# Attention and mixture-of-experts block on one core: row sums moved between buffers, normalising on GpSimd, long projections in two parts

## The reference

```python
q = X @ Wq.T + bq ; k = ctx @ Wk.T + bk ; v = ctx @ Wv.T + bv
w = softmax(where(masks, -inf, q k / sqrt(16)))        # 32 heads, 256 x 256
x = x + tanh(g_xattn) * ((w v) @ Wo.T + bo)            # X is the layernorm of x
t = layernorm(x)
shared = (silu(t @ S1.T) * (t @ S3.T)) @ S2.T          # S1, S3: 512 to 256; S2 back
scores = sigmoid(t @ gate.T) ; top 2 of 8 experts (with bias)
x = x + tanh(g_ffn) * (shared + sum of the two chosen experts, bf16)
```

## Time and profile before

| | |
|---|---|
| median of 3 runs | 863.16 us (861.75 to 866.41) |
| the profiled execution | 858.97 us, span 856.9 us |
| mean granted clock of TensorE | 0.877 of 2.4 GHz |
| busy TensorE / VectorE / ScalarE / GpSimd | 693.1 / 469.0 / 291.4 / 68.7 us |
| first scores of body 0 | 67.5 us from the span's start |
| first VectorE multiply L817 of bodies 1 to 8 | 159.1, 230.1, 301.3, 369.0, 440.5, 511.5, 573.9, 632.3 us |
| expert phase | 669 to 857 us |

### The profile page before, as it was taken

How to read it: one execution, slowest core, us unless ns; L and a number is a source line. 1 busy time by engine, 2 the same in 40 slices (tenths; PEclk the granted TensorE clock), 3 DMA queues, 4 the chain that set the end, 5 groups by cost and what they waited for, 6 DMA issues and landing times. The chain is left out here.

```text
span 856.9 us, 14813 instructions
## 1 busy us (share of the span) xinstructions
PE 693.1 (81%) x4417; PEld 480.3 (56%) x4417; DVE 469.0 (55%) x1041; ACT 291.4 (34%) x601; POOL 68.7 (8%) x100
## 2 busy tenths in 40 slices
PE   0436999699599789869959969989637799999998
PEld 0335758477377568648737747657326344444443
DVE  4417665368458467555836846564223455555554
ACT  1121454244333344433524433443201333333332
POOL 7400001001001000100100100000102000000000
PEclk9965979789799989978979988859657899999999
DMA  4785464444535543553545462430236022222111
GB/s 149 171 228 103 109 159 125 80 103 138 113 97 119 130 100 102 147 86 85 155 81 119 118 129 49 103 84 26 90 74 111 25 62 62 62 62 62 49 48 50
DMA packets 65199, 84.84 MB, mean 99 GB/s; under 512 B 15176, under 2 KB 43664, under 8 KB 64912
## 3 DMA queue, kind: packets, MB, share of 16 engines
q1 hardware_dynamic: 61008, 77.58, 36.9%
q0 software_dynamic: 2304, 6.29, 3.9%
q10 hardware_dynamic: 1856, 0.57, 0.3%
HBM read 60.75 MB, written 29.70 MB: 106 GB/s over the span
## 5 line engine op out<-in xcount | busy, mean ns | idle before, releaser
L593 ACT ACTIVATE probs<-ps 128x512 f32<-128x512 f32 x256 | 147.2, 598 | 150.3 <-PE ps L936 149.9
L800 DVE TENSOR_REDUCE mx<-ps 128x2 f32<-128x512 f32 x256 | 172.6, 683 | 39.7 <-PE ps L917 39.3
L917 PE MATMUL ps<-kst,qst 65*128 65x256 f32 x512 | 127.9, 336 | 65.3 <-DVE mx L800 59.6
L917 PEld LDWEIGHTS ps<-kst,qst 65*128 65x128 f32 x512 | 96.4, 213 | 115.1 <-DVE mx L800 76.1
L1085 PE MATMUL ps_h<-w,q_sg 128*128 128x512 bf16 x512 | 132.8, 383 | 5.2 <-PEq L77 5.2
L936 PE MATMUL ps<-qst,kst 66*128 66x512 f32 x256 | 113.8, 447 | 2.3 <-ACT probs L593 1.1
L1136 DVE SCALAR_TENSOR_TENSOR hid<-ps_h,sc_in,up 128x256 bf16<-128x256 f32 x128 | 61.9, 484 | 87.1 <-ACT up L1126 86.1
L1126 ACT ACTIVATE up<-ps_h,sc_in 128x256 f32<-128x256 f32 x128 | 60.7, 475 | 120.1 <-PE ps_h L1085 120.1
L1085 PEld LDWEIGHTS ps_h<-w,q_sg 128*128 128x128 bf16 x512 | 49.9, 99 | 67.8 <-issue 10.5
L949 PE MATMUL psa<-probs,v_st 128*32 128x256 f32 x1024 | 77.9, 427 | 1.2 <-ACT probs L593 1.2
L1103 PE MATMUL ps_o<-probs,hidT 128*128 128x512 bf16 x256 | 76.2, 380 | 0.8 <-DVE hidT L1142 0.8
(11 more groups left out here) (126 smaller groups left out, 1071.7 us busy)
## 6 DMA issues: line engine op xcount, KB each, us to landing
qst<-q_d SPq DMA_DIRECT2D x96, 128.0 KB
q_d<-q_sg SPq DMA_DIRECT2D x32, 256.0 KB, 3.0
a_d<-a_sb SPq DMA_DIRECT2D x32, 256.0 KB, 2.2
x_n<-in_x SPq DMA_DIRECT2D x8, 512.0 KB, 4.0
c_raw<-in_ctxT SPq DMA_DIRECT2D x8, 512.0 KB, 3.4
w<-in_w13T POOLq DMA_DIRECT2D x8, 512.0 KB, 16.1
x<-in_x SPq DMA_DIRECT2D x8, 512.0 KB, 3.4
a_dn<-a_d SPq DMA_DIRECT2D x8, 512.0 KB
```

The source lines that it names most:

```text
L593: act.activation(probs[:, v % 8, :], ps2[v % 2][:, :, :].rearrange("p h q -> p (h q)"), ACT.Exp, scale=HD ** -0.5).then_inc(s_exp, 1)
L800: dve.tensor_reduce(mx[:, c % 2, 0:8 * NT].rearrange("p (h t) -> p h t", t=NT)[:, h:h + 2, w // 2], ps1[u % 2][:, :, :], AX_X, ALU.max)\
L917: last = pe.matmul(o[:, i, :], qst[0:ROW_MAX, c, h, t * P:t * P + P], kst[0:ROW_MAX, c, g % 2, :], start=(i == 0 or not masked), stop=not ...
```

## The change

Five things change together.

1. The sums no longer come back from DRAM. `move_sums` copies them from `a_sb` straight into `den`, two small transfers for each chunk, issued before that chunk's `store_a`.
2. The chain of normalising is cut in two halves of two chunks each. Half 0: values loaded and reciprocals stored in step 5, spread in step 9. Half 1: values in step 20, reciprocals (`store_r`, two transfers) in 21, spread in 23. VectorE takes reciprocals in steps 4 and 20.
3. The multiply and the low part move from VectorE to GpSimd (`normalise`, `low_values`), each on half the chunks; ScalarE takes the high part in steps 16 and 26.
4. H0, H1, G, W0 and W1 are each issued in two parts in different steps (`BEGUN` says where the first part stands). Both W parts wait for all of the normalised batch.
5. Items and transfers are put in other steps (K from 13 to 0, so the context is loaded a body earlier, at step 27; D, T and Q later; `store_q`, `load_stack` of the next batch at 24 instead of 22). Body 6 is written out, the loop runs over 2 to 5.

```diff
-PREP = [(11, "T0"), (12, "T1"), (13, "K"), (14, "Q0"), (16, "Q1"), (18, "Q2"), (20, "Q3"), (21, "V0"), (22, "V1")]
+PREP = [(0, "K"), (13, "T0"), (14, "T1"), (16, "Q0"), (18, "Q1"), (20, "Q2"), (21, "V0"), (22, "Q3"), (25, "V1")]
+FIRST = ["T0", "T1", "K", "Q0", "Q1", "Q2", "Q3", "V0", "V1"]
-TAIL = [(0, "MT3"), (29, "W0"), (30, "W1")]
-TAIL2 = [(1, "X0"), (2, "X1"), (4, "H0"), (5, "H1"), (6, "G"), (8, "D0"), (9, "D1")]
-ROUTE_AT, ROUTE_RATE = 9, 2
+TAIL = [(0, "MT3"), (29, "W0"), (31, "W1")]
+TAIL2 = [(1, "X0"), (2, "X1"), (5, "H0"), (8, "H1"), (10, "G"), (12, "D0"), (13, "D1")]
+BEGUN = {"H0": 4, "H1": 6, "G": 9, "W0": 28, "W1": 30}
+ROUTE_AT, ROUTE_RATE = 12, 2
...
+            def move_sums(b, c):
+                ready((s_aev, b * G + 2 * c + 2), (s_rd, b * 2 + c // 2 - 1))
+                for w in range(2):
+                    row = 32 * c + 16 * w
+                    sp.dma_start(den[row:row + 16, :], a_sb[HD:P:32, c % 2, w, :]).then_inc(s_den[c % 2], 16)
+
+            def load_values(b, h):
+                for i in range(2):
+                    ready((s_aw[i], b * 32 + 16 * h + 16))
+                ready((s_ln2, b * LN2))
+                sp.dma_start(a_dn[:, 2 * h:2 * h + 2, :].rearrange("p c q -> p (c q)"),
+                             a_d[b, :, 0:HD, 2 * L * h:2 * L * h + 2 * L]).then_inc(s_ar[h], 16)
...
+            def load_r(b, h):
+                ready((s_rw, b * 64 + 32 * h + 32), (s_ln2, b * LN2))
+                sp.dma_start(f(a_lo[:, 2 * h:2 * h + 2, :].rearrange("p c q -> p (c q)")),
+                             r_d[b, h].unsqueeze(1).broadcast_to([G, HD, 2 * L])).then_inc(s_rr[h], 16)
...
+            def normalise(b, h):
+                pool.wait_ge(s_rr[h], b * 16 + 16)
+                pool.wait_ge(s_ar[h], b * 16 + 16)
+                half = a_dn[:, 2 * h:2 * h + 2, :]
+                pool.tensor_tensor(half, half, a_lo[:, 2 * h:2 * h + 2, :].bitcast(F32), ALU.mult).then_inc(s_an, 1)
+
+            def low_values(b, h):
+                pool.wait_ge(s_ahi, b * 2 + h + 1)
+                pool.tensor_tensor(a_lo[:, 2 * h:2 * h + 2, :], a_dn[:, 2 * h:2 * h + 2, :],
+                                   a_hi[:, 2 * h:2 * h + 2, :].bitcast(F32), ALU.subtract).then_inc(s_alo, 1)
...
-                    if u in (27, 28) and prev:
-                        t = u - 27
-                        act.wait_ge(s_an, b * NT - NT + t + 1)
+                    if u in (16, 26) and prev:
+                        h = u // 26
+                        act.wait_ge(s_an, b * 2 - 2 + h + 1)
...
-                    pe.wait_ge(s_alo, b * NT + k + 1)
+                    if part == 0:
+                        pe.wait_ge(s_alo, b * 2 + 2)
...
+                            for name, begin in BEGUN.items():
+                                if begin == u and name in idx and not last:
+                                    item(name, b - 1 if name[0] == "W" else b - 2, idx[name], (par0 + par[name]) % 2, idx, 0)
```

More of the change, by code:

```diff
@@ L206, in attention_phase @@
         s_aw = [sem(f"s_aw{i}") for i in range(2)]
-        s_den = sem("s_den")
+        s_den = [sem(f"s_den{i}") for i in range(2)]
         s_rd = sem("s_rd")
         s_rw = sem("s_rw")
-        s_rr = sem("s_rr")
-        s_ar = sem("s_ar")
+        s_rr = [sem(f"s_rr{h}") for h in range(2)]
+        s_ar = [sem(f"s_ar{h}") for h in range(2)]
         s_an = sem("s_an")
@@ L429, in body @@
                         load_stack(b, 3)
-                    if u == 18 and prev:
-                        load_sums(b - 1)
+                    if prev and u in (5, 20):
+                        load_values(b - 1, u // 20)
+                    if prev and u in (5, 21):
+                        store_r(b - 1, u // 21)
+                    if prev and u in (9, 23):
+                        load_r(b - 1, u // 23)
                     if u == 17 and attn:
                         max_row(b, 1, idx)
[L434 to L440, removed]
+                    if nxt and u in (17, 19, 21, 23):
+                        store_q(b + 1, (u - 17) // 2, idx)
+                    if nxt and u == 24:
                         load_stack(b + 1, 0)
+                    if u == 27 and nxt and not (isinstance(b, int) and b == B - 2):
+                        load_context(b + 2)
                     if attn and u == 24:
+                        move_sums(b, 0)
                         store_a(b, 0)
@@ L807, in body @@
                         norm1(b + 1, u - 9)
[L808 to L818, removed]
-                    if u in (28, 29) and prev:
-                        t = u - 28
-                        dve.wait_ge(s_ahi, b * NT - NT + t + 1)
-                        dve.tensor_tensor(a_lo[:, :, t * P:t * P + P], a_dn[:, :, t * P:t * P + P],
-                                          a_hi[:, :, t * P:t * P + P].bitcast(F32), ALU.subtract).then_inc(s_alo, 1)
-                    if u in (6, 7) and old:
-                        h = u - 6
+                    if u in (4, 20) and prev:
+                        h = u // 20
+                        for i in range(2):
+                            dve.wait_ge(s_den[i], b * 64 - 64 + 32 * h + 32)
+                        wait(dve, s_rw, b * 64 - 128 + 32 * h + 32)
+                        dve.reciprocal(rden[64 * h:64 * h + 64, :], den[64 * h:64 * h + 64, :]).then_inc(s_rd, 1)
+                    if u in (7, 10) and old:
+                        h = u // 10
                         dve.wait_ge(s_ghi, b * HC - 2 * HC + h + 1)
@@ L828, in body @@
                             .then_inc(s_glo, 1)
+                    if u == 1 and old:
+                        norm2(b - 2, 1)
                     for name in at[u]:
@@ L846, in _, with split_mm @@
         def _(pe):
-            def split_mm(outp, a, w):
+            def split_mm(outp, a, w, part=None):
                 n = len(a[0])
-                for c in range(n):
+                for c in range(n) if part is None else range(part * n // 2, (part + 1) * n // 2):
                     for i, j in ((hi, hi), (hi, lo), (lo, hi)):
@@ L864, in plain_mm, with item @@
                 return last
-            def item(name, b, n, par, idx):
+            def item(name, b, n, par, idx, part=None):
                 m = psm[par]
-                wait(pe, s_free, n - 1)
+                if part != 1:
+                    wait(pe, s_free, n - 1)
                 k = int(name[-1]) if name[-1].isdigit() else 0
@@ L889, in item @@
                 elif name[0] == "W":
[L890 to L893 removed]
+                    if part == 0:
+                        pe.wait_ge(s_alo, b * 2 + 2)
+                        if isinstance(b, int) and b == 0:
+                            pe.wait_ge(s_wlo, N_W[2])
+                    last = split_mm(m[:, :], toks(a_hi, a_lo, k * P, k * P + P), cols(Wo, D, 0, D), part)
                 elif name[0] == "G":
[L895 to L896 removed]
+                    for t in (part,):
                         last = split_mm(m[:, t * E:t * E + E], toks(x_hi, x_lo, t * P, t * P + P), cols(Gt, E, 0, E))
                 elif name[0] == "H":
[L899 to L900 removed]
+                    if part == 0:
+                        pe.wait_ge(s_free, idx["X1"] + 1)
+                    for i, w in ((part, (S1, S3)[part]),):
                         last = split_mm(m[:, i * L:i * L + L], cols(w, HID, k * P, k * P + P), toks(x_hi, x_lo, 0, L))
@@ L904, in item @@
                     last = split_mm(m[:, :], toks(g_hi, g_lo, k * P, k * P + P, HC), cols(S2, D, 0, D, HC))
-                last.then_inc(s_item, 1)
+                if part != 0:
+                    last.then_inc(s_item, 1)
             def pass1(b, u, masked):
```

80 lines of the change are left out of this document (38 added, 42 removed).

## The result

The changed kernel takes 841.0 us (median of 4 runs, 839.3 to 845.7) against 864.8 us (4 runs, 861.8 to 866.7) before: a ratio of 0.974, interval 0.968 to 0.979. It is faster, as forecast, but by 24 us and not by 57, and 841 lies just outside the range of 773 to 840.

The account below looks back on a forecast made before the run. TensorE was taken to set the pace except in one hole per body; 67 - 24 + 8 + 5 + 4 - 3 = 57 us off the profiled 859.0 gave 802, about 806 us by the median, range 773 to 840.

Parts of the forecast that it names:

- term 2: Before W0: the new chain takes 16.8 us against 14 of TensorE work; wait 2.5 and clock 1.5 per body, 24 us back.
- Term 5: The ends: tail in body 8 gains 4 us; start in body 0 loses 3 us as K waits for its context.
- term 3: Evenness and gate item: 5 us less TensorE idle outside the hole, one clock fall after G less, 3 us; 8 us gained.
- Term 1: TensorE's hole before W0 and the slow matmuls after it go, 11.2 us in each of bodies 1 to 6: 67 us.
- Term 4: Body 7, with a short hole but the clock at half for 16.5 us and more: 5 us gained.
- A: Rival: the new chain is in time, no wait before W0; about 777 us, chance 0.22.
- C: Rival: each new wait before W0 is followed by 24 us at half clock; slower, about 875 us, chance 0.06.
- D: Rival: the hole only moves to step 0 of the next body, waiting for the stack; about 861 us, chance 0.04.
- B: Rival: GpSimd locks out VectorE, or the chain ends at its upper bounds; about 835 us, chance 0.20.

Follow-up runs that it names:

- e1: Changed kernel with W multiplying constant weights, so it waits for no chain, and ScalarE's high part of half 1 in step 29; output not the reference's: 790.9 us.
- e5: Changed kernel with the second half's reciprocals in VectorE's step 19 and their stores in SyncE's step 20, ahead of the load of the values: 827.2 us.
- e7: Changed kernel with the second half's multiply and low parts back on VectorE, the first half's left on GpSimd: 827.2 us.
- e15: Changed kernel with Q0 and Q1 moved from steps 16 and 18 to 18 and 19, so Q0 lies behind the last sums: 820.6 us.
- e3: Changed kernel with H0, H1, G, W0 and W1 issued whole in the step where they end, W0 thus waiting in step 29: 833.2 us.
- e2: Changed kernel with G's 24 matmuls streaming 256 columns of Wq instead of 8 gate columns; scores not the reference's: 819.3 us.
- e9: Changed kernel with the K item in step 3 instead of 0 and its store in step 5 instead of 2: 836.9 us.
- e6: The e3 kernel (whole items) with ScalarE's rounding of the second half in step 28 instead of 26: 834.5 us.
- e10: Changed kernel with W one step later: W0 begun in step 29 and ended in 30, W1 begun in 30 and ended in 31: 833.0 us.
- e13: Changed kernel with W one step later, as in e10, and ScalarE's rounding of the second half in step 28 instead of 26: 840.4 us.
- e11: Changed kernel with the edits of e5 and e7 together: 818.8 us.
- e16: Changed kernel with the edits of e5, e7, e9 and e15 together: 812.0 us.

## Why the prediction was wrong

The main mechanism was right: the hole goes, and a shorter wait for the same chain comes before W0. But terms 2 and 5 were mis-sized, and term 3 had the wrong sign. The spans up to W0 of body 7, with e1 as the kernel without the new wait; us gained:

| stretch | forecast | measured |
|---|---|---|
| bodies 2 to 6 without new wait | 5 x 11.2 + 5.7 = 61.7 | 352.4 - 305.6 = 46.8 |
| start and body 1 without it | 11.2 + 1.1 - 3 = 9.3 | 102.3 - 101.2 = 1.1 |
| body 7 | 5 + 1.1 = 6.1 | 62.4 - 58.3 = 4.1 |
| the new wait | -24 | -36.6 |
| tail | 4 | 3.2 |
| sum | 57.1 | 18.6, and 0.3 behind it |

The first row is 14.9 us short. By the busy times, 12.0 of them are small idles (term 3), and 3.3 are time of TensorE's own: 8.0 us of it went, where terms 1 and 3 had 11.4.

**Term 1, right.** The hole went whole: in five bodies 42.2 us of it and 5.0 before W0.

**Term 2, the wait, mis-sized.** The prediction put the chain at 16.8 us beside 14, wait 2.5, clock 1.5. The work beside it was right (14.8). The chain was 20.2 us in body 4 and 19.8 in the mean of bodies 2 to 6. By the rows of body 4 it took 6.8 us to the stores instead of 5.5: VectorE ended the reciprocals 5.1 us after the sums, not 4.1, and then `store_r` stood on SyncE behind `load_values` and `store_scores`. The stores' own landing fits (3.7, forecast 2 to 4). `load_r` took 6.4 us instead of 5 (6.0 in the mean of bodies 2 to 6, at the upper bound). It was a third faster than the whole array at the same place (9.1 to 9.7 us), but not half: the 6.8 us that the estimate halved is from body 7, where little else is in flight. There the half took 3.8 us:

```profile
554.65 0.66 SPq L378 DMA_DIRECT2D a_lo<-r_d  x1
...
558.45 1.27 POOL L509 TENSOR_TENSOR a_dn<-a_dn,a_lo 128x512 f32<-128x512 f32 x1 [3.32 <-DMA a_lo<-r_d]
```

GpSimd and ScalarE were right, 3.3 us. So the wait was 5.0 us in the mean; by e1 it costs 5.75 us net in each of the five bodies, 4.0 of it idle (1.0 of the wait only covers small idles) and 1.8 of clock. e5, e7 and e15 shorten the chain or lengthen the work beside it, and each gains.

**Term 3, evenness, wrong in sign; as large an error as term 2.** I counted 5 us less idle outside the hole, 3.6 of them in these five bodies. The small idles rose from 6.2 to 9.6 us there, and with no wait at all (e1) to 14.6. The rise has two parts. The waits before G and before the transposes, 4.0 and 3.4 us, stand in after and in e1 at the same size, so they do not come with the hole or the wait, but with the new places and parts of the items; for G, e3 shows it (1.7 us with whole items). The other 5.0 us come in e1 alone, 4.0 of them before `pass2` for the maximum rows. That TensorE meets these because the hole had let VectorE and the transfers catch up is argued, and no run isolates it. And e3 shows no gain by cutting the items. The fall after G was to come once less; it comes in bodies 2 to 8, all seven, where before body 4 had none. e2 puts it at 21.8 us in all.

**Term 4, nearly right**: 4.1 of 6.1.

**Term 5.** The tail was right, 3.2 of 4. The start was not: 9.1 us lost to body 1 (10.2 of hole and slow W0 gone, 1.1 gained) against 3. The upper bound of 5 held for the waits for the context, 4.7 us; the clock, 3.5 us more of the same matmuls, was not in the sum. The wait for the context (68.5 to 72.0 us) does not make it fall: it is down from 64 us on in after and from 65 before. What the changed kernel does is stay down for longer, and e9 halved the wait without changing that. The cause is open.

**Rivals.** A is shown wrong by the waits. C did not come: half clock covers 10 to 14 of the 67 us of a body. D did not come. B's number, 835, was nearest, by the chain at its upper bounds; its other half, GpSimd locking out VectorE, is seen but small. Timelines of GpSimd and VectorE in body 4:

```profile
348.97 1.30 POOL L513 TENSOR_TENSOR a_lo<-a_dn,a_hi 128x512 fp32r<-128x512 f32 x1 [10.04 <-ACT a_hi L653]
349.01 1.29 DVE L753 SCALAR_TENSOR_TENSOR sel<-keep,sel 128x16 f32<-128x16 f32 x1
```

Seven VectorE operations on at most 64 elements last over 1 us, 8.8 us in all; before there were five, 10.7 us.

**Left open.** Why the clock falls after G in every body now, what sets it at the start, and what brings the 5.0 us of small idles in e1.

## What to carry to other kernels

A chain of transfers is worth its length less the work that the waiting engine has beside it. So count that work in items, not in steps: here an empty step was worth 0.5 us, and one item moved across it 2.2 us, and moving the wait to another engine or step (e6, e10, e13) gained 8 us at most, which the intervals do not tell from nothing, while a shorter chain or longer work beside it gained in e5, e7, e11, e15 and e16. A hole in the bounding engine goes whole when its cause goes, but its length is no forecast of the gain: other waits come, here 8.4 us in five bodies with no wait left before W0. And when a transfer is cut in half, take its time from the same place in the loop, not from a quiet one.

## What the runs showed of the hardware

Two transfers of 4 KB from a few partitions (`den<-a_sb`) took SyncE 1.21 us to issue, two of 8 KB (`r_d<-rden`) 1.64 us, while one of 256 KB (`a_d<-a_sb`) took 0.43. A broadcast load of 256 KB (`a_lo<-r_d`) took 5.4 to 6.8 us in bodies 1 to 6 (half 1), 3.8 in body 7 and 4.2 in the tail, where less is under way; the one of 512 KB took 9.1 to 9.7, 6.8 and 7.8 us in the same three places before. G, 24 matmuls of 8 columns, was followed by 6.8 us at 1.2 GHz in all seven bodies of the changed kernel, and by no such stretch when its matmuls had 256 columns (e2). With G spread over three steps, stretches of 10 to 21 us at 1.2 GHz came where TensorE was under way 94 to 100% of the time.
